# Attention block on one core: the next image loaded in pieces, the norms' small passes on one tensor, q read back by head

## The reference, cut to what matters

```python
# x: (8, 256, 64, 64) float32
img = (x - mean_g) / sqrt(var_g + 1e-5)              # group norm, 32 groups of 8 channels, per image
q, k, v = split(einsum('bcxy,oc->boxy', img, w_qkv)) # 8 heads of 64, m = 64*64 pixels
k = softmax(k, axis=pixels)
context = einsum('ndm,nem->nde', k, v)
content = einsum('nde,ndm->nem', context, q)
Sx = einsum('ndxy,xid->nixy', q4, Px)                # Px[x, i] = rel_rows[i - x + 63]
Yh = einsum('nixy,neiy->nexy', Sx, v4)
Yh = batchnorm(Yh, over all images and heads) * gamma + beta
Sy = einsum('ndxy,yid->nixy', q4, Py)                # Py from rel_columns
rel = einsum('nixy,nexi->nexy', Sy, Yh)
out = x + einsum('bcxy,oc->boxy', content + rel, w_out) + b_out
```

## Time and profile before

| | us |
|---|---|
| median of 3 runs | 3025.26 |
| the profiled execution, its own time | 3016.12 |
| its span | 3014.0 |
| TensorE busy | 2656.9 (88%) |
| VectorE / ScalarE / GpSimd busy | 1875.2 / 1544.1 / 1248.7 |
| mean granted TensorE clock | 0.953 of full |

### The profile page before, as it was taken

How to read it: one execution, slowest core, us unless ns; L and a number is a source line. 1 busy time by engine, 2 the same in 40 slices (tenths; PEclk the granted TensorE clock), 3 DMA queues, 4 the chain that set the end, 5 groups by cost and what they waited for, 6 DMA issues and landing times. The chain is left out here.

```text
span 3014.0 us, 131462 instructions
## 1 busy us (share of the span) xinstructions
PE 2656.9 (88%) x61044; PEld 2127.2 (71%) x61044; DVE 1875.2 (62%) x2986; ACT 1544.1 (51%) x2884; POOL 1248.7 (41%) x557
## 2 busy tenths in 40 slices
PE   2999999999998998999989986887979888888889
PEld 1788787787787877878778775666666666666665
DVE  5567667676676676676675556655555555555553
ACT  1565565655656656566565553444443444344443
POOL 2244334424325335244253336544444444454641
PEclk9999999999999999999999997899999999999999
DMA  3233434425325235234235337767666766666663
GB/s 143 60 85 115 100 74 128 102 59 149 81 66 162 61 77 153 60 90 139 70 98 121 95 94 159 176 173 173 176 171 174 173 173 171 168 175 182 178 179 106
DMA packets 433042, 383.62 MB, mean 127 GB/s; under 512 B 297840, under 2 KB 364656, under 8 KB 430448
## 3 DMA queue, kind: packets, MB, share of 16 engines
q1 hardware_dynamic: 414064, 341.66, 44.1%
q10 hardware_dynamic: 18432, 33.56, 3.1%
HBM read 206.31 MB, written 168.82 MB: 124 GB/s over the span
## 5 line engine op out<-in xcount | busy, mean ns | idle before, releaser
L787 POOL TENSOR_TENSOR k_f<-k_f,negmax 128x1024 f32<-128x1024 f32 x128 | 303.4, 2399 | 851.7 <-DVE negmax L752 851.7
L430 PE MATMUL bank<-w_hi,x_hi 128*128 128x256 f16 x2048 | 576.6, 282 | 39.0 <-POOL x_lo L771 23.4
L430 PE MATMUL bank<-w_lo,x_hi 128*128 128x256 f16 x2048 | 570.7, 279 | 2.5 <-issue 2.5
L430 PE MATMUL bank<-w_hi,x_lo 128*128 128x256 f16 x2048 | 569.9, 278 | 0.3 <-issue 0.3
L1241 POOL TENSOR_TENSOR x_f<-x_f,y_norm_by 128x1024 f32<-128x1024 f32 x127 | 273.3, 2152 | 552.5 <-DMA x_f<-y_scratch 550.2
L697 DVE TENSOR_TENSOR v_lo<-bank,v_hi 128x256 f16<-128x256 f32 x512 | 213.5, 420 | 261.7 <-ACT v_hi L565 260.6
L564 ACT ACTIVATE k_f<-bank 128x256 f32<-128x256 f32 x512 | 199.5, 390 | 315.3 <-PE bank L430 314.3
L1205 DVE TENSOR_TENSOR o_lo<-bank,o_hi 128x512 f16<-128x512 f32 x256 | 167.0, 684 | 279.6 <-ACT o_hi L1117 279.2
L1015 PE MATMUL bank<-q,rc_both 128*64 128x64 f16 x4096 | 276.2, 245 | 64.6 <-DMA q<-q_scratch 32.7
L1117 ACT ACTIVATE o_hi<-bank 128x512 f16<-128x512 f32 x256 | 142.1, 594 | 370.7 <-PE bank L1046 370.7
L430 PEld LDWEIGHTS bank<-w_hi,x_hi 128*128 128x128 f16 x2048 | 297.5, 145 | 47.4 <-issue 23.5
(11 more groups left out here) (146 smaller groups left out, 8293.3 us busy)
## 6 DMA issues: line engine op xcount, KB each, us to landing
y_scratch<-yst SPq DMA_DIRECT2D x256, 256.0 KB, 3.8
x_f<-y_scratch SPq DMA_DIRECT2D x256, 256.0 KB, 5.3
q<-q_scratch SPq DMA_DIRECT2D x256, 256.0 KB, 4.7
x_f<-x SPq DMA_DIRECT2D x16, 2048.0 KB, 11.3
q_scratch<-q_hi SPq DMA_DIRECT2D x128, 256.0 KB, 3.4
q_scratch<-q_lo SPq DMA_DIRECT2D x128, 256.0 KB, 4.1
x_res<-x SPq DMA_DIRECT2D x128, 256.0 KB, 6.9
out<-x_res ACTq DMA_DIRECT2D x128, 256.0 KB, 3.3
```

The lines of the kernel that those rows point to most:

```text
L430: mm = pe.matmul(outs, lhs[a], rhs[m], start=first and n == 0, stop=last and n == 2, **kw)
L787: pool.tensor_tensor(kk, kk, negmax[:, :].unsqueeze(1).to_broadcast([P, 8, P]), ALU.add).then_inc(shifted, 1)
```

## The change

Three edits. (1) `x_f` of the next image is loaded in quarters of a chunk (512 KB each, 4 KB per partition): chunk 0 during head pair 0 and chunk 1 during head pair 1, at four points between the stores, with one semaphore for each chunk. (2) In `image_stats`, `gn_channels`, `gn_scale` and `gn_bias` the passes with two tensors in SBUF are written as `tensor_scalar`, one tensor with pointers to per-partition columns, one column at a time. Two passes of `gn_scale` over both columns stay. (3) `load_q` reads one of the two heads and half of x (2 KB runs) instead of both heads and a quarter of x (1 KB runs). The first half goes behind `ro` items 3 and 5, the second, both heads, behind item 7.

```diff
-                    dve.scalar_tensor_tensor(ymv[:, 1:2], ymv[:, 0:1], ymv[:, 0:1], ymv[:, 1:2],
-                                             ALU.mult, ALU.add).then_inc(y_stats, 1)
+                    dve.tensor_scalar(ymv[:, 1:2], ymv[:, 0:1], ymv[:, 0:1], ymv[:, 1:2],
+                                      ALU.mult, ALU.add).then_inc(y_stats, 1)
                     dve.wait_ge(y_stats, n + 3)
-                    dve.tensor_tensor(acc[:, :], acc[:, :], ymv[:, :], ALU.add).then_inc(y_stats, 1)
+                    for k in range(2):
+                        o = dve.tensor_scalar(acc[:, k:k + 1], acc[:, k:k + 1], ymv[:, k:k + 1], None, ALU.add)
+                    o.then_inc(y_stats, 1)
...
-                    dve.tensor_tensor(rstd[:, :], gs[:, :, 0], gs[:, :, 0], ALU.mult).then_inc(bn_done, 1)
-                    dve.wait_ge(bn_done, base + 2)
-                    dve.tensor_tensor(rstd[:, :], gs[:, :, 1], rstd[:, :], ALU.subtract).then_inc(bn_done, 1)
+                    for c in range(CC):
+                        dve.tensor_scalar(rstd[:, c:c + 1], gs[:, c, 0:1], gs[:, c, 0:1], gs[:, c, 1:2],
+                                          ALU.mult, ALU.subtract).then_inc(bn_done, 1)
                     dve.wait_ge(bn_done, base + 3)
-                    dve.tensor_scalar(rstd[:, :], rstd[:, :], 0.0, None, ALU.max).then_inc(bn_done, 1)
+                    dve.tensor_scalar(rstd[:, :], rstd[:, :], -1.0, 0.0, ALU.mult, ALU.max).then_inc(bn_done, 1)
                     dve.wait_ge(bn_done, base + 4)
                     dve.tensor_scalar(rstd[:, :], rstd[:, :], GN_EPS, None, ALU.add).then_inc(bn_done, 1)
...
-                load_x(b + 1)
+                load_x(b + 1, 0, 0)
...
+                        next_x(0)
                         store_ys(0, 1)
                         if hp < HP - 1:
                             store_q(0)
+                        next_x(1)
                         store_ys(2, 3)
...
-                                load_q(b, hp + 2, i // 2)
+                                if i in (3, 5):
+                                    load_q(b, hp + 2, 0, i // 2 - 1)
+                                if i == 7:
+                                    for h in range(2):
+                                        load_q(b, hp + 2, 1, h)
```

More of the change, by code:

```diff
@@ L155, in attention_kernel @@
         group = sb("group", [P, P], F32, p1)
-        x_in = sem("x_in", p1)
+        x_in = [sem(f"x_in{c}", p1) for c in range(CC)]
         with ExitStack() as st, nc.Block() as block:
@@ L183, in _ @@
                 for c in range(CC):
-                    sp.dma_start(x_f[:, c, :], x_chunks[0, c]).then_inc(x_in, 16)
+                    for k in range(4):
+                        s = slice(k * (PIX // 4), (k + 1) * (PIX // 4))
+                        sp.dma_start(x_f[:, c, s], x_chunks[0, c][:, s]).then_inc(x_in[c], 16)
                 for g in range(2):
@@ L356, in _, with load_x @@
             def _(sp):
-                def load_x(index):
-                    for c in range(CC):
-                        sp.dma_start(x_f[:, c, :], x_chunks[index, c]).then_inc(x_in, 16)
+                def load_x(index, c, quarter):
+                    s = slice(quarter * XC, quarter * XC + XC)
+                    sp.dma_start(x_f[:, c, s], x_chunks[index, c][:, s]).then_inc(x_in[c], 16)
                 sp.sem_inc(q_st, 128)
@@ L400, in store_ys, with next_x @@
                                     store_y(b, hp - 1, i)
+                        def next_x(quarter):
+                            if order is not final_turn and hp < CC and (hp, quarter) != (0, 0):
+                                load_x(b + 1, hp, quarter)
+                        next_x(0)
                         store_ys(0, 1)
@@ L407, in turn @@
                             store_context(b * HP + (hp - 1))
+                        next_x(2)
                         store_ys(4, 5)
@@ L412, in turn @@
                         store_ys(6, 7)
+                        next_x(3)
                     if order is final_turn:
@@ L422, in _ @@
                     sp.wait_ge(y_st[s], 16 * (NT * YH // YST + 1))
-                sp.wait_ge(x_in, 16 * CC * NB)
+                for c in range(CC):
+                    sp.wait_ge(x_in[c], 64 * NB)
             @block.tensor
@@ L630, in gn_stats @@
                     if k % 8 == 0:
-                        dve.wait_ge(x_in, nth * 16 * CC + 16 * CC)
+                        dve.wait_ge(x_in[c], nth * 64 + 64)
                     dve.bn_stats(bn6[:, c, j, :], x_f[:, c, j * 512:j * 512 + 512]).then_inc(bn_done, 1)
@@ L641, in gn_channels @@
                     for c in range(CC):
-                        dve.scalar_tensor_tensor(mv[:, c, 1:2], mv[:, c, 0:1], mv[:, c, 0:1], mv[:, c, 1:2],
-                                                 ALU.mult, ALU.add).then_inc(bn_done, 1)
+                        dve.tensor_scalar(mv[:, c, 1:2], mv[:, c, 0:1], mv[:, c, 0:1], mv[:, c, 1:2],
+                                          ALU.mult, ALU.add).then_inc(bn_done, 1)
                 def gn_scale(nth):
@@ L660, in gn_bias @@
                     dve.wait_ge(gn_root, nth + 1)
-                    dve.tensor_tensor(nbias[:, :], gs[:, :, 0], rstd[:, :], ALU.mult).then_inc(bn_done, 1)
-                    dve.wait_ge(bn_done, base + 6)
-                    dve.tensor_scalar(nbias[:, :], nbias[:, :], -1.0, None, ALU.mult).then_inc(bn_done, 1)
+                    for c in range(CC):
+                        dve.tensor_scalar(nbias[:, c:c + 1], gs[:, c, 0:1], rstd[:, c:c + 1], -1.0,
+                                          ALU.mult, ALU.mult).then_inc(bn_done, 1)
                 def gn_apply(nth, k):
@@ L922, in _, with load_q @@
             def _(sp):
-                def load_q(b, hp, c):
-                    x0 = c * XY
+                def load_q(b, hp, part_of_x, h):
+                    a = H // XB // 2
                     for part in range(2):
                         rows = slice(part * 64, part * 64 + 64)
-                        sp.dma_start(q2[rows, hp % 2, :, :, x0 // XB:(x0 + XY) // XB, :, :].rearrange("p h g a y x -> p (h g) (a y x)"),
-                                     q_dram[b * HP + hp].rearrange("l d h g n -> l d (h g) n")
-                                     [part, :, :, x0 * HALF:(x0 + XY) * HALF]).then_inc(q_in[hp % 2], 16)
+                        sp.dma_start(q2[rows, hp % 2, h, :, part_of_x * a:(part_of_x + 1) * a, :, :].rearrange("p g a y x -> p g (a y x)"),
+                                     q_dram[b * HP + hp, part, :, h, :, part_of_x * (PIX // 4):(part_of_x + 1) * (PIX // 4)]
+                                     ).then_inc(q_in[hp % 2], 16)
                 def load_context(b, hp):
@@ L944, in _ @@
                     sp.sem_inc(out_st[s], 16)
-                for c in range(YC):
-                    load_q(0, 0, c)
+                for k in range(4):
+                    load_q(0, 0, k // 2, k % 2)
                 load_context(0, 0)
-                for c in range(YC):
-                    load_q(0, 1, c)
+                for k in range(4):
+                    load_q(0, 1, k // 2, k % 2)
                 sp.wait_ge(cb_lo_done, 1)
@@ L1009, in turn @@
                             if i == 0:
-                                pe.wait_ge(q_in[hp % 2], (b * 2 + (hp // 2 + 1)) * (32 * YC))
+                                pe.wait_ge(q_in[hp % 2], (b * 2 + (hp // 2 + 1)) * 128)
                             for j in range(8):
```

## The result

The changed kernel takes 3041.01 us (median of 15 runs, 3030.12 to 3044.27), the kernel before 3025.3 us on the same chip (15 runs). One run of before at 3681 us is left out of the comparison. The ratio is 1.0055, 95% interval 1.0039 to 1.0071: some 17 us slower. That lies in my range (2999 to 3046), above the point of 3030, and on the side to which I had given 0.32; the likeliest case said +4.5 us.

What follows compares the result with a forecast made beforehand. The prediction took TensorE (PE) as the bound, busy 2656.9 of 3014.0 us. Terms -15 - 2.5 + 18 + 4 = +4.5 us on the profiled 3016.1 gave 3020.6, plus 9.1 to the runs' median, say 3030; range 2999 to 3046.

Steps and rivals of the forecast that it cites:

- `image_stats`, one column: First stage: one-column passes don't wait for GpSimd, shortening TensorE's gaps and raising its clock; -15 us (bounds -8 and -20).
- `gn_scale`, two columns stay: First stage: the two remaining two-column passes still wait for GpSimd, only two passes' 0.2 us each saved; -2.5 us.
- q: longer waits: Second stage: the last q piece, now 1 MB, makes TensorE wait 2.1 us longer at most places; 30 us.
- q: given back in issue waits: Second stage: 40% of the longer q wait returns because TensorE's instructions go on arriving while it waits.
- q, in time: Second stage: net cost of the longer q waits after what is given back; +18 us (bounds +5 and +38).
- x in quarters: First stage: 49 quarter loads among the stores, where TensorE has issue gaps; +4 us (bounds -3 and +12).
- Rival B: Second stage: the q wait is paid in full, 30 us, and the x quarters cost 12; 3050 us, chance 0.17.
- 0.3 us at 14 turns: First stage: the step pricing the x quarters among the stores, giving +4 us.
- My sign for it: First stage: TensorE's "issue" waits over 55 us would put the loss on the x quarters.
- The argument from the rate of wide passes: VectorE: passes taking two columns at once need the path GpSimd holds and wait; one-column passes can't.
- rival A: `gn_scale`: two-column passes are too short to wait for GpSimd, -29 us there; 3003 us, chance 0.26.
- rival D: Norms: one-column passes wait for GpSimd as well, so their rewriting does nothing; +22 us, 3047, chance 0.03.

Runs made afterwards that it cites:

- norms_only: The kernel before with only the norms' passes rewritten to one SBUF tensor and one column, two two-column passes of `gn_scale` staying; 3007.13 us, ratio 0.9943.
- x_only: The kernel before with only the x loads changed, to quarters issued among the stores; 3037.43 us, ratio 1.0036.
- after_x_burst: The changed kernel with its eight x quarters issued together, where the kernel before has its burst; 3013.52 us, ratio 0.9986.
- copies_dense: The kernel before plus 49 unneeded 512 KB DRAM-to-DRAM copies, issued at the points of the changed kernel's x quarters; 3040.78 us, ratio 1.0068.
- copies_burst: The kernel before plus 49 unneeded 512 KB DRAM-to-DRAM copies, issued right behind the x burst, beside wide `kv` matmuls; 3023.53 us, ratio 1.0004.
- norms_one_col: The kernel before with the norms' passes rewritten and the last two two-column passes of `gn_scale` also done by column; 3000.14 us, ratio 0.9907.
- q_late_1k: The kernel before with q in its 1 KB runs, issued as late as in the changed kernel; 3026.22 and, repeated, 3029.19 us, ratios 1.0012 and 1.0022.
- norms_q_early: norms_one_col with each q piece issued once the content matmuls of its `ro` pair have read q, some 1.5 us earlier; 2997.42 us, ratio 0.9926.
- q_only: The kernel before with only the q loads changed, by head in halves of x; 3033.55 and, repeated, 3036.27 us, ratios 1.0021 and 1.0047.

## Why the prediction was right or wrong

| term | forecast, us | measured, us |
|---|---|---|
| `image_stats`, one column | -15 | -17 for both (norms_only) |
| `gn_scale`, two columns stay | -2.5 | |
| q: longer waits | +30 | +45 |
| q: given back in issue waits | -12 | -32 |
| q, in time | +18 | +6 to +14 |
| x in quarters | +4 (-3 to +12) | +11 (x_only); +21 between after_x_burst and the changed kernel |
| sum | +4.5 | +16.6 by the ratio (0 to +8 from the edits alone) |

**The range held and the point was on the wrong side.** I called no change the likeliest, at +4.5 us; it is +17. The errors of the terms have opposite signs, q too dear and x too cheap, so that the sum came out nearer than its parts: that it stayed in the range is in part luck. Rival B's time (3050) is about as near as mine (3030), but not its mechanism: the issue waits of the second stage fell by 32 us, where B had them stay. Only its 12 us for the x quarters was nearer the truth than my 4. One reading was too wide as well: the chain of the earlier trace rows that I took for TensorE's work almost alone covers 39% of the span, and all of its lines are in the second stage; for the first stage it says nothing.

**The step that failed is edit 1's**, "0.3 us at 14 turns". I saw that the quarters go among the stores, where the issue waits are, and then priced them far below what a burst on a busy DMA costs there: 21 to 26 us more of issue waits in 49 loads are 0.4 to 0.5 us a load, of the 1.2 us for which, by my estimate, each keeps the DMA engines busy; in time it is 11 us in x_only, 21 in copies_dense and 21 in after_x_burst against the changed kernel, 0.2 to 0.4 us a load. Two of the three are above my upper bound of 12 us. copies_dense and copies_burst show that the price is for the place and not for x. My sign for it, issue waits of the first stage over 55 us, was no sign: I had read 47.7 us off one line, and over all lines the kernel before has 57.2 already.

**Edit 2 was right in its steps**: which passes wait and for how long, which TensorE wait goes (14.3 to 0.6 us; 2.4 in norms_only, where I had said 3) and which stays, and the sum of 17.5 us, of it 11 of waits and 4 through the clock for `image_stats` (measured in norms_only, for both parts of the edit: 14.2 us of waits and 5.4 of busy time). The argument from the rate of wide passes held down to two columns, as norms_one_col shows; rival A (3003) is refuted by L669 and L671, rival D by L635 and L639. The two pages of the Trainium skill that I had set beside it, Vector Engine (DVE) Microarchitecture Reference, section Performance modes, and SBUF — State Buffer, section Who interferes with whom, agree: 1.55 and 2.28 us with two columns, 0.15 with one. What they speak against is only half of the edit, and going to one column there as well was worth some 7 to 11 us, not the 26.5 between my two bounds: I hadn't counted that in this stretch other waits take the place of the one that goes (107.4 and 101.7 us in sum for 106.8).

**Edit 3 was right in kind and off in both sizes.** The wait behind the last piece is longer than I computed: in the example of the earlier trace rows it was 2.76 us, and it is now

```profile
2479.79 2.56 SPq L943 DMA_DIRECT2D q<-q_scratch  x4
```

```profile
2488.36 0.26 PE L1034 MATMUL bank<-q,rc_both 128*64 128x64 f16 x2 [5.71 <-DMA q<-q_scratch]
```

8.6 us from issue to use instead of 5.6. The DMA engines were 30% busy until 2482 and nearly full from then on, at 254, 198 and 257 GB/s in three windows of 2 us; the first two rows:

```profile
2480.00:2482.00 2.00, 2.00 (x80) 1.53 (x78) 1.40 (x3) 1.85 (x3) 1.92 (x2) 1.00 0.30 90
2482.00:2484.00 2.00, 0.65 (x42) 0.54 (x34) 2.00 (x1) 1.32 (x4) 2.00 (x2) 1.00 1.06 254
```

The bandwidth was as forecast. But from 2480 to 2488 it comes to 1.6 MB, and the piece has 1.05: other transfers went with it. The four Yh loads issued behind the piece, from 2484.52 on, may be among them; whether they lengthen the wait was not tested. And more came back than the 40% that I gave: in q_late_1k all but 4 to 7 us of 45 to 49. What I can say of the second stage is that waits for q and issue waits together move much less than the waits for q: 150 to 162 us in the seven profiles with before's second stage, 164 to 175 in the six with the late piece, 158 in norms_q_early, for waits for q of some 31, 80 and 18 us.

**Open.** q_only's stage was 1215.4 and 1213.2 us and that of the changed kernel and after_x_burst, with edit 3 too, 1217.2 and 1218.4; q_late_1k's was 1203.7 and 1211.5, with nearly equal waits for q. So the 2 KB runs by head may cost some us by themselves, but stages of one and the same code lay between 1197.4 and 1209.7 us, and the intervals of the times overlap. What an "issue" wait is made of the profile does not show. That TensorE's instructions arrive late while the DMA engines are busy fits these runs (unneeded copies lengthen the issue waits, waiting for q shortens them, and nearly all stand at items of many short matmuls), but no run measured the arrival. The Trainium skill, Runtime: NRT & Kernel Launch, section Instruction fetch mechanics, has each engine fetch its instructions by a DMA queue of its own and calls the cost of going from one block of them to the next mostly hidden. The page of the profile has such a queue ("instruction", 479 packets, 7.85 MB, before and after alike). If these waits are that fetch, "mostly hidden" doesn't hold here: before the change 57 us of the first stage and 119 of the second were not hidden. No run here shows that they are.

## What to carry to other kernels

Price a transfer by what runs beside it when it is in flight: the same 512 KB cost nothing measurable beside wide matmuls and 0.2 to 0.4 us beside stretches of many small ones, so a burst may be better than an even spread. A wait that a change takes away or adds in a stretch with many issue waits can count for less than half in the time (45 us of longer waits for q made 4 to 14 us); look at the sum of all waits, and at more than one profile, since one and the same code had 80.5 and 61.1 us of issue waits. And small VectorE passes beside a busy GpSimd should read one SBUF tensor and write one column at a time: here passes of 0.15 us had become waits of 1.5 to 2.3, twice in each `gn_scale`.

## What the runs showed of the hardware

A `tensor_scalar` over two float32 columns in SBUF waits for the running GpSimd instruction (1.55 and 2.28 us), the same over one column doesn't (0.149 us, norms_one_col). A pointer to a column as a scalar adds some 60 ns each: 0.149 us with none, 0.209 with one (L639), 0.268 to 0.273 with two (L666, L635), each over one column. Loads of q over 64 partitions moved 227 to 231 GB/s in 1 KB runs (four windows of 2 us from 1820 on, one of them in the earlier trace rows) and hardly more in 2 KB runs, 232 to 242 GB/s in the changed kernel (four windows from 1826 on).
